# Adapters loaded half by SyncE's and half by GpSimd's queue, and the bias kept on 128 partitions, in a fused conditioning and mixture layer on one core

## What is computed

```python
# conditioning layer, per batch row b (8 rows of 128 tokens, 512 features)
base_out = x @ W.T + b
A, Bm    = lora_As[adapter_mapping], lora_Bs[adapter_mapping]      # 1 of 32 adapters, rank 16
y        = base_out + (x @ A) @ Bm * 2
# second layer
base   = y @ W_base.T + b_base
logits = y @ W_router.T                                            # 8 experts
rw, sel = top_k(logits, 2); rw = softmax(rw); w = weights of the two, 0 for the others
h      = einsum(y, A_expert)                                       # 8 experts x rank 16
out    = x + base + einsum(h, w, B_expert) * 2
```

## Time and profile before

| | us |
|---|---|
| median of three runs | 68.00 (67.62 to 68.04) |
| the profiled execution | 66.77 |
| its span, first to last instruction | 65.0 |
| PE busy | 61.4 |
| DVE busy | 36.4 |
| ACT busy | 21.2 |
| POOL busy | 16.6 |

### The profile page before, as it was taken

How to read it: one execution, slowest core, us unless ns; L and a number is a source line. 1 busy time by engine, 2 the same in 40 slices (tenths; PEclk the granted TensorE clock), 3 DMA queues, 4 the chain that set the end, 5 groups by cost and what they waited for, 6 DMA issues and landing times.

```text
span 65.0 us, 1179 instructions
## 1 busy us (share of the span) xinstructions
PE 61.4 (94%) x422; PEld 60.4 (93%) x422; DVE 36.4 (56%) x105; ACT 21.2 (33%) x46; POOL 16.6 (26%) x30
## 2 busy tenths in 40 slices
PE   5999999999999999999999999999999999999930
PEld 5979999999989999998999999999999999999920
DVE  0058899995899076125825576002768354957320
ACT  0674537064999299145112100020201040020000
POOL 6820000000089998777370000010100000000000
PEclk9999999999999999999999999999999999999999
DMA  0799997525999304245559879810044000013632
GB/s 0 220 419 417 241 311 212 186 78 131 203 308 392 136 0 102 61 105 131 125 120 347 252 238 405 315 59 0 0 161 161 10 0 0 0 77 126 218 136 88
DMA packets 5865, 10.55 MB, mean 162 GB/s; under 512 B 731, under 2 KB 2523, under 8 KB 5860
## 3 DMA queue, kind: packets, MB, share of 16 engines
q1 hardware_dynamic: 5570, 10.15, 48.7%
q10 hardware_dynamic: 290, 0.33, 1.5%
HBM read 7.37 MB, written 2.10 MB: 146 GB/s over the span
## 4 chain that ended last, share of the span: by engine, by line
PE 90%; ACT 3%; ACTq 2%; DVE 1%; issue 0%
PE ps L673 26%; PE ps L581 23%; PE ps L685 19%; PE ps L733 9%; PE ps L642 6%; PE ps L708 2%; ACT L342 2%; PE ps L713 2%; PE ps L696 1%; PE ps L719 1%; ACTq L345 1%; ACTq L346 1%; ACT wt_hi L342 1%; DVE xn L534 1%; PE ps L652 0%
## 5 line engine op out<-in xcount | busy, mean ns | idle before, releaser
L673 PE MATMUL ps<-am,x_hi 128*128 128x384 f32 x64 | 16.6, 340 | 0.0
L685 PE MATMUL ps<-bm,x_hi 128*128 128x280 f32 x64 | 13.0, 297 | 0.0
L673 PEld LDWEIGHTS ps<-am,x_hi 128*128 128x128 f32 x64 | 11.4, 188 | 0.0
L673 PE MATMUL ps<-am,x_lo 128*128 128x384 f32 x32 | 10.8, 337 | 0.0
L309 POOL TENSOR_TENSOR x_lo<-xt,x_hi 128x512 fp32r<-128x512 f32 x8 | 10.2, 1288 | 0.0
L685 PEld LDWEIGHTS ps<-bm,x_hi 128*128 128x128 f32 x64 | 10.1, 188 | 0.0
L685 PE MATMUL ps<-bm,x_lo 128*128 128x280 f32 x32 | 9.3, 290 | 0.0
L534 DVE TENSOR_TENSOR xn<-ps,xn 128x280 f32<-128x280 f32 (+1 forms) x16 | 6.1, 419 | 2.7 <-PE ps L733 2.6
L581 PE MATMUL ps<-wt_hi 128*128 128x280 f32 (+1 forms) x32 | 7.3, 325 | 0.2 <-ACT wt_hi L342 0.2
L581 PE MATMUL ps<-wt_lo,wt_hi 128*128 128x280 f32 (+1 forms) x32 | 6.9, 312 | 0.0
L581 PE MATMUL ps<-wt_hi,wt_lo 128*128 128x280 f32 (+1 forms) x32 | 6.5, 310 | 0.0
(11 more groups left out here) (72 smaller groups left out, 95.4 us busy)
## 6 DMA issues: line engine op xcount, KB each, us to landing
xt<-x_t SPq DMA_DIRECT2D x4, 512.0 KB, 5.7
xn<-x_n SPq DMA_DIRECT2D x4, 512.0 KB, 6.3
out_n<-xn SPq DMA_DIRECT2D x7, 256.0 KB, 2.0
wt<-w_chunks SPq DMA_DIRECT2D x3, 582.0 KB, 4.1
g_st<-g_hl SPq DMA_DIRECT2D x12, 81.0 KB, 2.1
ab<-adapters SPq DMA_DIRECT2D x8, 64.0 KB, 2.4
wt<-w_chunks SPq DMA_DIRECT2D x2, 128.0 KB, 2.9
btt<-b_t SPq DMA_DIRECT2D x1, 256.0 KB, 5.2
```

What stands on the lines that cost most here:

```text
L673: last = mm(a_bank(b)[:, 0:R + WA], v[:, p, i, tok], am[:, i, level, at:at + R + WA], start=(i == 0 and n == 0), stop=False, skip_group_ch ...
L685: mm(b_bank(b)[:, 0:QB], v[:, p, i, tok], bm[:, i, level, :], start=(i == 0 and n == 0), stop=False, skip_group_check=True)
```

## The change

Four edits. (1) SP issues adapters 0 to 3 only, with xt of the first two rows ahead of adapters 2 and 3; POOL's queue issues adapters 4 to 7, behind its constants, with a semaphore of its own (`abp_in`). (2) ACT makes `bs_hi` and `as_hl` before `x_high(0)` and not behind the bias; it waits for both semaphores there. (3) The bias sum stays on 128 partitions: DVE's copy and addition are gone, ACT and DVE make high and low parts of 128 x 648 (`bsum_hl`), and PE sums with four products in place of two. (4) On DVE `bs_lo` stands ahead of the bias' low part, and POOL's low part of A waits for the bias' low part. The tile `c_hl` is gone; C's high and low rows are put into row 0 of `bsum_hl`.

```diff
@@ SP
             adapter(1)
-            adapter(2)
             sp.dma_start(xt[:, 0], x[:, 0]).then_inc(x_in[0], 16)
-            for b in range(3, NB):
+            for b in range(2, BY_SP):
                 adapter(b)
@@ POOL
+            pool.wait_ge(idx_in, 16)
+            for b in range(BY_SP, NB):
+                slot = pool.value_load(idx_sb[0:1, b:b + 1], min_val=0, max_val=SLOTS - 1)
+                pool.dma_start(ab[:, b].rearrange("p c k r -> p (c k r)"),
+                               tbl[bass.ds(slot, 1)].rearrange("s p n -> (s p) n")).then_inc(abp_in, 16)
...
-            pool.wait_ge(bs_lo_done, 1)
+            pool.wait_ge(bsum_lo_done, 1)
             pool.wait_ge(ab_hi_done, 2)
@@ ACT
-            x_high(0)
-            act.wait_ge(halves_done, 1)
-            hi(bsum_st[0:HP], bsum[0:HP]).then_inc(bsum_hi_done, 1)
-            act.wait_ge(ab_in, 16 * NB)
+            act.wait_ge(ab_in, 16 * BY_SP)
+            act.wait_ge(abp_in, 16 * (NB - BY_SP))
             hi(bs_hi[:].rearrange("p k b r -> p b k r"), ab[:, :, 1]).then_inc(ab_hi_done, 1)
             hi(as_hl[:, :, :, 0, :], ab[:, :, 0]).then_inc(ab_hi_done, 1)
+            x_high(0)
+            act.wait_ge(bsum_done, KB)
+            hi(bsum_hl[:, 0], bsum[:]).then_inc(bsum_hi_done, 1)
@@ DVE
-            dve.wait_ge(bsum_done, KB)
-            nc.vector.tensor_copy(upper, bsum[HP:P]).then_inc(upper_done, 1)
-            dve.wait_ge(upper_done, 1)
-            nc.vector.tensor_tensor(bsum[0:HP], bsum[0:HP], upper, ALU.add).then_inc(halves_done, 1)
-            dve.wait_ge(bsum_hi_done, 1)
-            lo(bsum_st[HP:P], bsum[0:HP], bsum_st[0:HP]).then_inc(bsum_lo_done, 1)
             dve.wait_ge(ab_hi_done, 1)
             lo(bs_lo[:].rearrange("p k b r -> p b k r"), ab[:, :, 1],
                bs_hi[:].rearrange("p k b r -> p b k r")).then_inc(bs_lo_done, 1)
+            dve.wait_ge(bsum_hi_done, 1)
+            lo(bsum_hl[:, 1], bsum[:], bsum_hl[:, 0]).then_inc(bsum_lo_done, 1)
@@ PE
             for s, c in enumerate(COLS):
-                last = mm(ps[:, C_BANK + s, 0:c.stop - c.start], ones_r[:], bsum_st[:, c], start=True, stop=True)
+                for i in range(2):
+                    last = mm(ps[:, C_BANK + s, 0:c.stop - c.start], ones_r[:], bsum_hl[:, i, c],
+                              start=(i == 0), stop=(i == 1))
```

More of the change, by code:

```diff
@@ L45 @@
 AHEAD = 4
-HP = P // 2
+BY_SP = 4
 CH = D + WC
@@ L100, in build @@
         bsum = sb("bsum", [P, WC])
-        bsum_st = sb("bsum_st", [P, WC], F32R)
-        c_hl = sb("c_hl", [1, 2, WC], F32R)
+        bsum_hl = sb("bsum_hl", [P, 2, WC], F32R)
         h_stack = sb("h_stack", [P, PAIRS, 2 * HSTEP])
@@ L113, in build @@
         hw = sb("hw", [P, PAIRS, 2, P])
-        upper = hw[0:HP].rearrange("p a t c -> p (a t c)")[:, 0:WC]
         hw_hi = sb("hw_hi", [P, NB, P], F32R)
@@ L159, in build @@
         ab_in = sem("ab_in")
+        abp_in = sem("abp_in")
         x_in = [sem(f"x_in{p}") for p in range(PAIRS)]
@@ L189, in build @@
         bsum_done = sem("bsum_done")
-        upper_done = sem("upper_done")
-        halves_done = sem("halves_done")
         bsum_hi_done = sem("bsum_hi_done")
@@ L270, in _ @@
                         sp.dma_start(g_st[CROW + i:CROW + i + 1, :, :].bitcast(F32),
-                                     c_hl[0:1, i:i + 1, :].bitcast(F32).to_broadcast([1, PAIRS, WC])
+                                     bsum_hl[0:1, i:i + 1, :].bitcast(F32).to_broadcast([1, PAIRS, WC])
                                      ).then_inc(cst_in, 16)
@@ L385, in _ @@
             for s, c in enumerate(COLS):
-                hi(c_hl[0:1, 0, c], ps[0:1, C_BANK + s, 0:c.stop - c.start]).then_inc(c_hi_done, 1)
+                hi(bsum_hl[0:1, 0, c], ps[0:1, C_BANK + s, 0:c.stop - c.start]).then_inc(c_hi_done, 1)
             x_high(2)
@@ L473, in _ @@
                 dve.wait_ge(c_hi_done, s + 1)
-                lo(c_hl[0:1, 1, c], ps[0:1, C_BANK + s, 0:c.stop - c.start],
-                   c_hl[0:1, 0, c]).then_inc(c_lo_done, 1)
+                lo(bsum_hl[0:1, 1, c], ps[0:1, C_BANK + s, 0:c.stop - c.start],
+                   bsum_hl[0:1, 0, c]).then_inc(c_lo_done, 1)
             dve.wait_ge(bt_hi_done, 1)
```

## The result

| | before | the change |
|---|---|---|
| median of 20 runs each, us | 68.00 (66.89 to 68.33) | 68.06 (67.55 to 68.80) |
| profiled execution, us | 66.77 | 68.01 |
| its span, us | 65.0 | 65.8 |
| outside its span, us | 1.77 | 2.21 |
| DVE busy, us | 36.4 | 35.2 |

What follows compares the result with a forecast made beforehand. PE was taken as the bound, busy 58.27 of 58.28 us. +0.29 for C and -0.22 for the stop gave +0.07 us; with 1.23 from profiled execution to median, 68.1 us, range 67.5 to 69.2.

Steps and rivals of the forecast that it cites:

- the stop: PE's wait at the start of G, behind M, for DVE's low part of `am`: 0.22 us, to be gained.
- signs of being wrong: PE idle over 0.15 us ahead of G, `bs_hi` starting after 13.9, or PE waiting at a new place.
- A: Time when all adapters have landed: forecast 12.9 us, in time for G if at most 13.9.
- rival 1: POOL's adapters land after 13.9, ACT's queue is late and PE idles ahead of G: 69.6 us, chance 0.18.
- The bias on DVE and ACT: 0 on PE: Dropping DVE's copy and addition lies under M's products: 0 on PE if M's evictions are in time.
- C's cost: Four products in place of two for C on PE, with nothing to hide them: +0.29 us.
- The rule A + 4.7: DVE's `am` ends 4.7 us after the adapters are complete; each microsecond past the 13.9 limit costs PE one.
- Rival 3: Preparing or closing POOL's queue adds 0.9 us outside the span: 69.0 us, chance 0.04.
- The port rule: DVE's copy at 6.1 us blocks POOL's descriptor writing: fourth landing 0.42 us later, at 13.3; the sum stays 68.1.

Runs made afterwards that it cites:

- the second profile: The kernel before, unchanged, run again for another profile and each run's span: 68.03 us, 1.002 of before; weight chunk 1 landed at 7.34 us.
- without the fold: The kernel before without DVE's copy and addition, so half of the bias sum is left out, two products for C: 66.83 us, 0.983 of before.
- the change with all by SP: The changed kernel with all eight adapters issued by SP, none by POOL, ACT's new order kept: 68.88 us, 1.013 of before.
- the fold by POOL: Against the kernel before: ACT copies the bias sum's upper half, POOL adds it to the lower, high and low parts come later; adapters by SP: 68.51 us, 1.008.
- the kernel that only reads the slots: Bias kept on 128 partitions with four products, SP issuing all adapters; POOL also reads four slots without issuing transfers: 66.98 us, 0.985 of before.
- the bias edit alone: The kernel before with only the bias kept on 128 partitions and four products for C, all adapters by SP: 67.23 and 67.56 us, 0.992 over both.

## Why the prediction was right, and where it was not

The time, 68.06 against 68.1, and "no change" came out, but by luck: the sum, +0.29 for C and -0.22 for the stop, is not what happened. One of its own signs of being wrong came true (`bs_hi` started at 14.69, after 13.9), and most of what it said would be seen was not: the first eviction of M at 17.42 and not 16.3, the low part of `am` ended at 19.19 and not before 18.6, G at 19.38 and not 18.75, the later stages 0.7 to 0.8 us later and not 0.07, the span 65.8 and not 65.1. By its own rule an A of 14.7 is 0.8 us late, the condition of its rival 1. PE did not wait all the same, since in that execution M's end was itself 0.63 us later. The steps:

- **The choice of what to sum from failed.** The prediction read one execution of 66.77 us and carried the 1.23 us to the median over as a constant, as if it lay outside the kernel's work. Outside the span are 1.78 us in the median of before's runs; the 1.2 us are in the span (66.2 against 65.0) and were a wait of PE for DVE ahead of G. The sentence "in the part that the change touches there is one such place" was right; its size, 0.22 us, was that of a rare execution. In the second profile it is 1.15 us of idle time, and 1.4 counted as the 0.22 was.
- **"The bias on DVE and ACT: 0 on PE" failed.** The two DVE instructions lie on the chain of the second profile; without the fold 1.1 us go, and with C's products paid 0.4 to 0.7 remain.
- **C's cost held.** Forecast +0.29; 0.59 against 0.29 us in the chain.
- **The adapters' landing was mis-sized.** A was 14.7 in place of 12.9. POOL's issue is cheap, 0.54 us, but all landings take 4.5 us in the median. Two queues issue the same bytes sooner, onto engines that were already 0.95 busy: the last issue moved from 14.0 to 10.0 us, the last landing only from 15.9 (the change with all by SP) to 14.7. That the full engines are the reason is likely, not shown.
- **The rule A + 4.7 and its price held**, as A + 4.5 in two kernels, and 1.33 us of idle PE in the one that was behind the limit.
- **Rival 3 was half right.** 0.4 to 0.5 us outside the span came with POOL's adapters (forecast as a rival: 0.9, chance 0.04), but not from having a queue: one transfer costs none.
- **M was taken as fixed.** The prediction read one pitch for all products of a width, and summed nothing for M. Its first eight products have another, 0.24 us in place of 0.13 for a varying stretch, and that alone made M 0.5 us longer in the change's profile, more than any term of the sum.
- **The start was taken as fixed too.** Nothing allowed for the first instructions standing 0.12 us later and the first pieces of the weights landing 0.2 to 0.8 us later. The runs show it with POOL's run-time transfers and don't show why; M's start moved by 0.1 to 0.3 us.

The port rule that I weighed, from the Trainium skill, "SBUF — State Buffer", "Who interferes with whom", was aimed at a copy of DVE, which cost nothing visible: in the change that copy ran from 7.35 to 7.78 us, and the issue that POOL began beside it at 7.45 took 0.54 us, as its others did (0.53 to 0.68). Whether the transfer's landing was held isn't shown. Another sentence of that section, that a DVE instruction with two SBUF inputs contends with a GpSimd instruction that reads SBUF, is what the fold by POOL shows: 1.92 us in place of 0.83.

**What stays open.** Why weight chunk 1 lands at 5.9 to 6.4 us in some profiled executions and at 6.9 to 7.8 in most. Why POOL's transfers at run-time addresses delay the start and the first weights, and add 0.4 to 0.5 us outside the span. Why the first products of M run at about half their later rate for a while, and why the kernel that only reads the slots was faster than the bias edit alone. The fold by POOL also has 2.02 us outside, with no transfer of POOL's at all, so what lies outside is not a matter of POOL's queue alone.

## What to carry to other kernels

Look at the profiled execution's own time beside the median before you sum from it: where they differ by more than the effects in question, the profile may be of a rare execution, and a second one can show a different engine on the path. An edit that takes work off an engine behind the first loads is worth its time when the loads are late, even if one profile shows it idle there. A second queue brings transfers in by less than it issues them sooner: here 4.0 us at the issue were 1.3 at the landing, with the DMA engines 0.95 busy. Time the landing, not the issue. And when a forecast is met, compare its signs too: here the time agreed and the timeline did not.

## What was not expected of the hardware

- Four 64 KB gathers issued by POOL at addresses read at run time cost 0.6 to 0.9 us in all, of which 0.4 to 0.5 outside the span and 0.12 ahead of the first data; a single one, of 256 KB at a fixed address, cost 0, and four at fixed addresses 0.23 outside and nothing in the whole time against the bias edit on the same chip.
- A POOL transfer's issue takes 0.54 us against SP's 0.35, but the pitch is nearly the same, 1.15 and 1.10 us, since reading the slot is the larger part on both.
- M's first 280-column products had a pitch of 0.24 us in place of 0.13 for a stretch that differs from execution to execution (1.35 to 2.05 us to the first product of 368 columns), at a granted clock that reads 1.00.
- DVE's subtraction of two SBUF tiles took 1.92 us beside POOL's subtraction and 0.83 alone; with one operand in PSUM it was not slowed.
